# Moving the two layer-norm rows of a fused decoder block from DVE to ACT

## The reference

```
x = layernorm(x + self_attention(x))         # 16 heads of 64, causal, odd reshape of heads and tokens
x = layernorm(x + cross_attention(x, ctx))   # 16 heads of 16, 77 context rows, mask
x = layernorm(x + moe(x))                    # 8 experts, top 2, capacity 1280, exact gelu
layernorm(v) = (v - mean(v)) / sqrt(var(v) + 1e-5)
```

## Time and profile before

| | |
|---|---|
| median of the times shown | 1653.96 us (1651.42 to 1655.74) |
| profiled execution, its own time | 1652.24 us |
| its span | 1650.5 us |
| PE busy | 1388.9 us, 84% |
| DVE busy | 1240.6 us, 75% |
| ACT busy | 1014.9 us, 61% |
| POOL busy | 725.9 us, 44% |
| mean granted TensorE clock | 0.939 of full speed |

### The profile page before, as it was taken

One profiled execution on the slowest core, in us unless ns is written; L12 is line 12 of the kernel. 1 busy time (PEld: TensorE's weight loads), 2 busy tenths in 40 slices (PEclk: granted clock), 3 DMA queues, 4 the chain that ended last, 5 costly groups with the idle time before them and its releaser, 6 DMA issues. The chain is left out here.

```text
span 1650.5 us, 50248 instructions
## 1 busy us (share of the span) xinstructions
PE 1388.9 (84%) x18194; PEld 1188.9 (72%) x18194; DVE 1240.6 (75%) x2833; ACT 1014.9 (61%) x2581; POOL 725.9 (44%) x918
## 2 busy tenths in 40 slices
PE   0799999999999999999999999750499999999930
PEld 0578888888888888888888887630388888888820
DVE  4578998998898998999999898638655555555536
ACT  3566878878788888888888767510144444444426
POOL 1134464564564564465465543420134344434325
PEclk9899999999999999999999999855699999999975
DMA  6434443443444434344344232009211111111147
GB/s 164 140 97 132 146 132 106 128 131 107 115 117 121 121 110 135 108 124 135 103 128 135 72 86 70 8 13 395 113 47 47 49 47 47 48 50 48 46 153 261
DMA packets 138988, 178.97 MB, mean 108 GB/s; under 512 B 78846, under 2 KB 110718, under 8 KB 134272
## 3 DMA queue, kind: packets, MB, share of 16 engines
q1 hardware_dynamic: 127616, 153.71, 30.8%
q0 software_dynamic: 6912, 17.84, 3.5%
q10 hardware_dynamic: 4224, 4.19, 0.7%
HBM read 93.92 MB, written 66.06 MB: 97 GB/s over the span
## 5 line engine op out<-in xcount | busy, mean ns | idle before, releaser
L1486 PE MATMUL ps_e<-xt,wres 128*128 128x128 f16 x3456 | 359.6, 220 | 0.2 <-issue 0.2
L1486 PEld LDWEIGHTS ps_e<-xt,wres 128*128 x3456 | 292.2, 98 | 73.3 <-issue 0.8
L1535 ACT ACTIVATE act_g<-ps_e,b 128x128 f32<-128x128 f32 x576 | 164.1, 368 | 227.2 <-PE ps_e L1486 118.2
L1493 PE MATMUL ps_e<-wres,g_hi 128*128 x576 | 217.5, 379 | 1.0 <-DVE g_lo L1565 1.0
L649 ACT ACTIVATE probs<-ps,nbias 128x128 f32<-128x128 f32 (+1 forms) x512 | 187.4, 417 | 8.3
L656 ACT ACTIVATE pt_hi<-ps 128x384 f16<-128x384 f32 x256 | 125.0, 488 | 102.7 <-PE ps L415 101.1
L1445 POOL DMA_INDIRECT z_scr<-e_y,dst_i x72 | 86.3, 1198 | 220.6 <-DVE e_y L1556 220.6
L813 DVE TENSOR_REDUCE nmax<-ps 128x1 f32<-128x128 f32 (+1 forms) x512 | 156.4, 346 | 26.0 <-PE ps L407 25.4
L1495 PE MATMUL ps_e<-wres,g_lo 128*128 x576 | 157.0, 273 | 0.0
L1553 DVE SCALAR_TENSOR_TENSOR e_y<-ps_e,b 128x256 f32<-128x256 f32 x72 | 30.6, 424 | 157.6 <-PE ps_e L1495 153.3
L1036 POOL TENSOR_TENSOR o_st<-o_norm,o_st 128x256 f16<-128x256 f32 x128 | 85.7, 669 | 144.0 <-ACT o_st L664 144.0
(11 more groups left out here) (257 smaller groups left out, 4596.0 us busy)
## 6 DMA issues: line engine op xcount, KB each, us to landing
piece<-in_moe_w SPq DMA_DIRECT2D x24, 768.0 KB, 5.7
w_scr<-piece_pair SPq DMA_DIRECT2D x24, 768.0 KB, 4.1
wres<-w_scr SPq DMA_DIRECT2D x18, 1024.0 KB, 22.3
v_scr<-v_tok SPq DMA_DIRECT2D x32, 512.0 KB, 2.6
v_pos<-v_scr SPq DMA_DIRECT2D x32, 512.0 KB, 4.5
k_pair<-k_pair SPq DMA_DIRECT2D x32, 512.0 KB, 4.4
z_scr<-zero SPq DMA_DIRECT2D x32, 256.0 KB, 3.5
f_z<-z_scr SPq DMA_DIRECT2D x8, 1024.0 KB, 12.7
```

Of the source, the lines that this page charges most:

```text
L1486: last = mm(out, w(c * FF + f * P, b, P), xt[:, t % 2, a, c], start=(m == 0), stop=(m == 5))
L1493: mm(out[:, 0:2 * D], g_hi[:, t % G_BUFS, f], w(KC * FF + f * D, 0, 2 * D), start=(f == 0), stop=False, skip_group_check=True)
L1535: nc.scalar.activation(act_g[:, k % 2, f], ps[:, 3 + 2 * (k % 2) + f // 4, (f % 4) * P:(f % 4 + 1) * P], ACT.Gelu, bias=bias[:, f:f + 1], ...
```

## The change

The row of the first norm and that of the second are taken out of DVE's queue and put into ACT's, as one activation each, `Identity(scale * y + bias)` with `scale = rstd` and `bias = -mean * rstd`, both read per partition from SBUF. POOL computes the bias: two more instructions of one column for each norm, `neg_mean` and `offset`. `var_eps` and `neg_mean` don't wait for each other; `rstd` waits for both, `offset` for `rstd`, and the row on ACT for `offset`. On ACT the first row stands between `pt(s, 2)` and `exps(s, 3)`, the second between `q2_hi` and `o_high(s, 1)`. DVE gets two new waits, on the previous tile's row, before it writes `y1` and `y2` again.

```diff
+    neg_mean = sb("neg_mean", [P, 2], F32)
+    offset = sb("offset", [P, 2], F32)
...
 ACT:
+        def first_norm(t):
+            p = t % 2
+            act.wait_ge(s_rstd1, 2 * t + 2)
+            nc.scalar.activation(x1[:, p], y1[:], ACT.Identity, bias=offset[:, 0:1], scale=rstd[:, 0:1]).then_inc(s_x1, 1)
+        def second_norm(t):
+            p = t % 2
+            act.wait_ge(s_rstd2, 2 * t + 2)
+            if since(t, 2):
+                act.wait_ge(s_out_x2[p], 16 * half(t))
+                act.wait_ge(s_x2_lo, t - 1)
+            nc.scalar.activation(x2[:, p], y2[:], ACT.Identity, bias=offset[:, 1:2], scale=rstd[:, 1:2]).then_inc(s_x2, 1)
...
             if has(s):
                 pt(s, 2)
+            if has(s - 1):
+                first_norm(s - 1)
+            if has(s):
                 exps(s, 3)
...
             if has(s - 1):
                 stage_c(s - 1, 3)
+            if has(s - 2):
+                second_norm(s - 2)
             if has(s):
                 o_high(s, 1)
...
 DVE:
-        def first_norm(t):
-            dve.wait_ge(s_rstd1, t + 1)
-            nc.vector.tensor_scalar(x1[:, p], y1[:], mv[:, 0, 0:1], rstd[:, 0:1], ALU.subtract, ALU.mult).then_inc(s_x1, 1)
-        def second_norm(t):
...
-            nc.vector.tensor_scalar(x2[:, p], y2[:], mv[:, 1, 0:1], rstd[:, 1:2], ALU.subtract, ALU.mult).then_inc(s_x2, 1)
...
+                if since(t, 1):
+                    dve.wait_ge(s_x1, t)
                 stt(out=y1[:], ...
+                if since(t, 1):
+                    dve.wait_ge(s_x2, t)
                 stt(out=y2[:], ...
...
 POOL:
             nc.gpsimd.tensor_tensor(var_eps[:, ln:ln + 1], mv[:, ln, 1:2], eps[:], ALU.add).then_inc(s_var, 1)
-            pool.wait_ge(s_var, t + 1)
+            nc.gpsimd.tensor_scalar(neg_mean[:, ln:ln + 1], mv[:, ln, 0:1], -1.0, None, ALU.mult).then_inc(s_var, 1)
+            pool.wait_ge(s_var, 2 * t + 2)
             nc.gpsimd.tensor_tensor(rstd[:, ln:ln + 1], var_eps[:, ln:ln + 1], neg_half[:], ALU.pow).then_inc(s_rstd, 1)
+            pool.wait_ge(s_rstd, 2 * t + 1)
+            nc.gpsimd.tensor_tensor(offset[:, ln:ln + 1], neg_mean[:, ln:ln + 1], rstd[:, ln:ln + 1], ALU.mult).then_inc(s_rstd, 1)
```

More of the change, by code:

```diff
@@ L850, in predicated @@
             nc.vector.tensor_reduce(mx2[:], sm[:, p], AX.X, ALU.max).then_inc(s_mx2, 1)
-        def first_norm(t):
-            p = t % 2
-            dve.wait_ge(s_rstd1, t + 1)
-            nc.vector.tensor_scalar(x1[:, p], y1[:], mv[:, 0, 0:1], rstd[:, 0:1], ALU.subtract, ALU.mult).then_inc(s_x1, 1)
         def stage_c(t, g):
@@ L948, in step @@
                 pt(s, 2)
-            if has(s - 1):
-                first_norm(s - 1)
             if has(s - 2):
@@ L964, in step @@
                 stage_c(s - 1, 3)
-            if has(s - 2):
-                second_norm(s - 2)
             if has(s):
```

## The result

| | before | after |
|---|---|---|
| median | 1653.78 us (4 runs, 1651.42 to 1655.74) | 1688.42 us (4 runs, 1685.92 to 1690.53) |
| profiled execution, its span | 1650.5 us | 1686.8 us |
| PE busy | 1388.9 us | 1385.8 us, 82% |
| DVE busy | 1240.6 us | 1207.0 us, 72% |
| ACT busy | 1014.9 us | 1045.4 us, 62% |

The change makes the kernel slower: ratio 1.0198, 95% interval 1.0177 to 1.0220, or 34.6 us by the medians. Forecast were 1685 us, with 1666 to 1703 as the range. DVE lost 33.6 us of work, ACT gained 30.5, and neither number says where the time went.

A forecast was written before the change was run, and what follows sets the result against it. No one engine was taken to bound the whole step; DVE bounds its second half. 30.0 us over steps 1 to 31 plus 0.6 twice for draining, 31 on 1652.24, gave 1683.5, stated as 1685 us, range 1666 to 1703.

The forecast's parts named there:

- The bound: Attention step of 31.65 us: DVE bounds the second half; in the first half the engines hand over with tenths to spare.
- POOL and ACT: First norm, even step: neg_mean and offset 0.19 us each on POOL; ACT row 0.58 us, holding its queue for 0.48.
- (d): Rival on ACT: Identity evicts the exponential's table, four loads a step, 164 us more, 1818 us; chance 0.01.
- The path: Late group-3 exponentials on ACT make PE's group-4 scores 1.47 (even) and 1.74 us (odd) late, x1_lo 1.22.
- The slack before the masked copy: On DVE after PE's cross scores: 0.18 us (even) and 0.33 (odd) absorb lateness, leaving 1.04 and 0.90 a step.
- the pattern: Steps 1 to 31, 15 even and 16 odd: 15 x 1.04 + 16 x 0.90 = 30.0 us more.
- draining: Two last steps: the chain from mean to row is exposed, costing 0.6 us twice.
- (a): Rival: DVE's freed 2.36 us in two steps comes through, ACT's wait hidden; -38 us, 1616 us; chance 0.09.
- (b): Rival: gain and price cancel if slack between x1_lo and the cross scores exceeds 1 us; about 1655 us; chance 0.07.
- (c): Rival: PE's stall is passed on in full, 1.47 and 1.74 us a step, PE becoming the bound; 1704 us; chance 0.13.
- at nothing: Second norm's row on ACT after q2_hi: no wait, its 0.48 us covered by pt(s, 4) waiting for PE's transposes.
- The clock: TensorE clock, at 0.98 of 2.4 GHz: a lower one was possible, unpriced and left to the range's upper end.

The follow-up runs named there:

- behind_exps: The changed kernel with the first norm's row on ACT placed behind the group-3 exponentials instead of ahead of them; 1654.39 us, ratio 0.9991.
- no_offset: The changed kernel without neg_mean and offset on POOL; both rows use a constant bias, so the mean is not subtracted; 1672.78 us, ratio 1.0092.
- early_mv: The changed kernel with the first norm's aggregation moved ahead of the group-3 maxima on DVE; 1684.19 us, ratio 1.0179.
- work_first: The kernel before plus one unneeded row on ACT, at the place of the first norm's row; 1655.15 us, ratio 0.9997.
- only_first: The changed kernel with only the first norm's row on ACT, the second still on DVE; 1705.41 us, ratio 1.0290.
- work_only: The kernel before plus two unneeded rows on ACT, at the change's two places, DVE and POOL as before; 1665.19 us, ratio 1.0069.
- second_wait: The kernel before with only the second norm's row on ACT, and POOL's second pair of context products waiting for DVE's first row; 1643.84 us, ratio 0.9920.
- second_split: As second_wait, but POOL computes the second norm's scale and offset between the two products, not behind both; 1638.33 us, ratio 0.9895.

## Why the prediction was right

The forecast, its sign and its size held (1685 against 1688.42), and so did the mechanism, step by step.

*The bound.* DVE is full only in the second half of a step. Right: relieved of 33.6 us, it waits for the scores for 61.0 us between 200 and 1000 us. `behind_exps` shows that the price lies in the place ahead of the exponentials, `no_offset` and `early_mv` that the chain the row waits for is paid at full rate, and `work_first` that the row without the wait is free.

*POOL and ACT.* From the mean's start to the row's, 1.54 us were forecast (571.67 to 573.21) and 591.86 - 590.28 = 1.58 measured; `neg_mean` was 0.23 and not 0.19, which moved `rstd` by 0.04. The row was 0.60, not 0.58, and holds ACT for 0.51, not 0.48. No table load came: rival (d) is dead.

*The path.* PE's scores were to start 1.47 and 1.74 late. Measured from the mean, 593.37 - 590.28 = 3.09 against 573.22 - 571.67 = 1.55 before: 1.54, and odd 626.61 - 623.26 = 3.35 against 605.02 - 603.48 = 1.54: 1.81. `x1_lo` was to be 1.22 late and was 4.71 - 3.40 = 1.31 in the even step.

*The slack before the masked copy* is the term that was mis-sized. From the end of the cross scores to the start of the copy it is 579.01 - 578.79 = 0.22 us in the even step and 611.23 - 610.86 = 0.37 in the odd one; I took 0.18 and 0.33 of it as slack, which leaves 0.04 for the hand-over. But in the changed kernel, where the hand-over does bind, it takes 598.87 - (598.43 + 0.29) = 0.15, and 0.15 in the odd step too (632.11 less the end at 631.96). The real slack was 0.07 and 0.22. Behind the copy 0.08 us came back, most of it in a gap before the next `pt_lo` that I had overlooked in saying that DVE runs there without one (580.85 to 581.26 before, 600.71 to 601.06 now). The cross scores end 1.32 us late in both kinds of step, so the even step grows by 1.32 - 0.07 - 0.08 = 1.17 by these rows (1.18 by the ruler) and the odd one by 1.32 - 0.22 - 0.08 = 1.02. Against the forecast a step has 0.10 more lateness and 0.11 less slack, and the 0.08 back: this is the difference between 30.0 us and 15 x 1.18 + 16 x 1.02 = 34.0.

*The span* grew by 36.3 us, and the pieces outside the pattern are not small. The first mean comes 1.7 us later (99.2, now 100.8). From it to the next is 33.53 us and was 30.63, so 2.9 more where the pattern has about 1. The next 29 steps have the pattern, 15 x 1.18 + 14 x 1.02 = 32.0, less the 4.3 of the three steps that the clock lengthened before. At the end the two last intervals, to the last first-norm mean and to the last second-norm mean, take 34.88 and 29.94 us in place of 33.20 and 28.69, 2.9 more, where the prediction had 1.2 for draining; behind it another 1.0 follows. Together 36.2. The prediction had no term for the first interval, the start and the clock, and there it was lucky: what the clock gave back covers two thirds of the 6 us that the start and the two ends cost beyond its sum.

*The rivals.* (a), DVE's gain coming through, was wrong as a forecast of the change, but it has a core: the second row alone gives some of it, 6.7 us by its steps. (b) fails on the slack. (c), the stall passed on in full, comes near in size in `only_first`, 1.49 and 1.34 a step, but not by PE: there DVE keeps its second row and, coming later, meets POOL with it in both kinds of step (its median is 555 ns, before 409). So the second row's move softened the loss by 0.31 and 0.32 a step; by way of the slack I had given it 0.18 and 0.33. I had priced that move "at nothing" on ACT, and that was right in the change; `work_only` shows that it depends on what POOL does beside it.

*The clock.* I gave it no price. It stood at 0.99 after [0.98 in rows 1], so it cost the change nothing, though PE was less busy. By the missing long steps it gave back some 4 us; in two experiments it cost as much.

## What to carry to other kernels

Before an instruction goes to a less busy engine, look at what stands behind it in that engine's queue. Ahead of an urgent instruction a cheap row delays everything behind it by its wait and its own length (here 1.3 and 0.5 us on ACT, and 1.3 us of it arrived in the step), and one place further back the same row costs 0.3 us a step; `second_wait` and `second_split` show the same at another place. Of two like moves, make each alone: by their steps one was worth -7 us here and the other +44, and only their sum was seen. Where the clock can move by itself, compare undisturbed steps and not medians alone: a version that looked 0.4% faster had won 1 us in its steps. A gap between the end of one engine's work and the start of the next engine's isn't slack until the hand-over, 0.15 us here, is taken off; read it where it binds.

## What the runs showed of the hardware that was not expected

TensorE's clock can fall inside a stretch in which PE looks the same in all steps. In the trace of before three steps are longer by 1.44 us, in `only_first` and `work_only` six each, in the changed kernel and in eight of the experiments none of that size. Cut into stretches of 4 us from 112 to 1008 us, the traces show a granted clock of 0.75 or less in each of these steps, and 0.97 or more in all the others. One of those of before, in busy time by stretch:

```profile
420.00:424.00 4.00, 3.54 (x53) 3.06 (x52) 3.93 (x12) 3.29 (x9) 3.12 (x4) 1.00 0.84 192
424.00:428.00 4.00, 3.54 (x28) 3.15 (x27) 3.84 (x8) 3.60 (x9) 3.66 (x6) 0.70 0.02 7
```

The granted clock of 0.70 is the mean of a stretch with part of it at the full 2.4 GHz and part at 1.2; ahead of it PE was busy for 3.54 of 4 us. Kernels whose steps differ by tenths of a microsecond have between none and six of these, and at 1.44 us each a handful of them is as much as many a change is worth. What starts a fall wasn't settled here.

The stall between DVE and POOL has a sharp edge. The same 0.41 us row on DVE takes 0.55, 0.90 or 1.3 us by what POOL runs at that moment, and an edit on a third engine (a spare row on ACT) was enough to move it from 0.41 to 0.90. Its length can be read off POOL's timeline: in each of these cases the row ends 0.14 to 0.16 us after the POOL instruction that it meets. In the kernel before the 1.30 us row ends at 606.18 and the first product beside it (604.78, 1.26 us long) at 606.04, and the second norm's 0.55 us row at 610.31, behind this split of o, which ends at 610.17:

```profile
609.50 0.67 POOL L1036 TENSOR_TENSOR o_st<-o_norm,o_st 128x256 f16<-128x256 f32 x1 [0.27 <-ACT o_st L664]
```

In `work_only` the pair is 583.99 and 583.84, in `only_first` 573.71 and 573.55.
